# Causal mask of the second score pass: a TensorE mask product or a GpSimd selection on the exponentials

## The chip, the cores and the metric

The kernel runs on one core of one Trainium2 chip. The metric is the device time of one execution in microseconds (us), from launch to the last store. The engines are named as the profile names them: PE is TensorE's matmul, PEld its weight load, DVE is VectorE, ACT is ScalarE, POOL is GpSimd, SP is the DMA queue of SyncE. "L1170" is line 1170 of the kernel before.

## The reference, cut to what matters

The reference is a macaron block on 8 sequences of 512 tokens with 512 features: half a routed feed-forward layer (32 experts, 4 per token), causal attention with 16 heads of 32 features and an ALiBi bias, and half the same feed-forward layer again. The change touches attention alone:

```
x = x + 0.5 * ffn(layernorm(x))
scores = einsum('bqhd,bkhd->bhqk', q, k) * scale + alibi_bias
scores = where(tril(ones(S, S)), scores, -1e9)     # a query sees no later key
p = softmax(scores, axis=-1)
x = x + (p @ v) @ Wout.T + b_out
x = x + 0.5 * ffn(layernorm(x))
```

A "future entry" is a pair of a query and a later key. With 512 tokens cut into tiles of 128, only the diagonal 128x128 square of a key tile's scores holds both kinds; tiles wholly in the future are not computed.

## The kernel before, in words

The program has four stages, one after the other: the routing, the first feed-forward layer, attention (`attend`, L758), the second feed-forward layer. Only `attend` is touched.

**Work units.** `attend` goes through the batches b = 0 to 7 (seven in a hardware loop, the last one written out after it) and in each through four groups g = 0 to 3 of four heads (HG = 4), 32 units in all (u = 4b + g). A unit makes two passes over its scores.

- The first pass (`scores_row`, L1107) computes scores with the queries on the partitions, into `psa`. It is done for the unit after the running one. DVE adds the mask and takes each row's maximum (`maximum`, L1389), PE turns the maxima (`turn_maxima`, L1113), DVE negates them, and two DMAs on ACT's queue (`maxima`, L1278) put them as two more rows into `stq`, so that the second pass subtracts them in the product itself. PE waits for these rows (`s_mr`) at the start of a unit.
- The second pass (`attention`, L1164 to L1187) computes the scores turned, with the keys on the partitions, into `psb`, which has two halves. It runs over the key tiles kt = 0 to 3 and in each over the heads j = 0 to 3, so over n = 4 kt + j = 0 to 15. The tile of kt has the queries from kt * 128 on: 512, 384, 256 and 128 columns. Two products make a tile: the scores (L1168, fp32r, 100 rows), and the mask product (L1170, bf16, 128x128x128: an identity times a matrix with -1e30 at the future entries), which is added to the first 128 columns, the diagonal square. The mask product's semaphore increment (`s_b`) tells ACT, which takes the exponential (`probability`, L1262) of the whole tile into `pt[kt][:, j, :]` and increments `s_e`.
- Between them PE's order is written out by hand: after the scores of n stand, by the tables `A_AT`, `K_AT` and `X_AT`, the next unit's first pass, a quarter of the projection of the keys of the unit after that (`project`, L1080), and in g = 1 the turning of the next batch's rows.

**Two readers of the exponentials.** Both matter here.

- PE's `context(u, g, kt)` (L1128 to L1138) multiplies the values with `pt[kt]` into `psc`, four heads at a time, and increments `s_pv`. It waits until the four exponentials of its key tile are there. It stands in PE's order after the scores of n = 6, 10, 14 for kt = 0, 1, 2 (that is, kt - 1 at j = 2), and after n = 15 for kt = 3.
- POOL's `add_rows(u)` (L994 to L1006) adds `pt[1]`, `pt[2]` and `pt[3]` into `pt[0]`, head by head: four additions of 128x384, four of 128x256, four of 128x128, in that order. The first waits for the context of kt = 0 (`s_pv`), since that reads the old `pt[0]`; each waits for its own exponential. The twelfth releases PE's `sums` (L1140 to L1147, through `s_z`), which adds over the partitions and so gives the softmax's denominators. `sums` of a unit stands in the next unit, behind the first quarter of the projection of the queries (3 matmuls), and for g = 3 behind `values(0)` (12 matmuls). ACT turns the sums into reciprocals (L1269, L1271), DVE multiplies (`normalise`, L1409), and POOL splits the result into a high and a low part (`split_context`, L989 and L991), in the next unit and before that unit's additions.

ACT's exponential n = 0 of a unit waits for the `sums` of the unit before, and the exponentials of kt > 0 for its last addition. After g = 3 POOL has four additions of the bias (L1012), the split, and the stores.

The lines on which it hangs:

```
for kt in range(1, TB):                                        # add_rows, POOL
    for j in range(HG):
        if kt == 1 and j == 0: g.wait_ge(s_pv, u * 4 + 5)
        g.wait_ge(s_e, u * 16 + (kt * HG + j + 2))
        g.tensor_tensor(pt[0][:, j, kt * P:S], ..., pt[kt][:, j, :], ALU.add).then_inc(s_z, 1)
...
pe.wait_ge(s_z, u * 12 + 13)                                   # sums, PE
```

Of the kernel before, what the change touches and what calls it, by code (L numbers as in the profile page):

```python
# [21 lines left out]
P = 128  # L22
ALU = mybir.AluOpType
# [9 lines left out]
B, S, H, HD = 8, 512, 16, 32  # L33
# [724 lines left out]
def attend(nc, tb, d):  # L758
# [5 lines left out]
    NG, HG, TB = H // 4, 4, S // P  # L764
# [11 lines left out]
    DONE_AT = {3: 0, 4: 1, 6: 2, 8: 3}  # L776
    ROW_AT, LOW_AT = {5: 0, 6: 1, 8: 2, 9: 3}, {12: 0, 13: 1, 14: 2, 15: 3}
    RY = TB

    def uses(last):  # L780

# [56 lines left out]
    with ExitStack() as c:  # L838
        sb = lambda n, shape, dt=F32: c.enter_context(nc.sbuf_tensor(f"a_{n}", shape, dt))
        ps = lambda n, shape: c.enter_context(nc.psum_tensor(f"a_{n}", shape, F32))  # L840
        sem = lambda n: c.enter_context(nc.semaphore(f"a_{n}"))
# [2 lines left out]
        wqkv = [sb(f"wqkv_{n}", [P, DC, CQ], F32R) for n in "hl"]  # L844
        wout = [sb(f"wout_{n}", [P, DC, D], F32R) for n in "hl"]
        bqk = sb("bqk", [P, 2 * DC])
        masks, causal = sb("masks", [P, 2, P], BF16), cst[:, C_MQ:C_MK + P].bitcast(BF16)

        stq, stk = sb("stq", [KROWS, 2 * HG, S], F32R), sb("stk", [KROWS, 2 * HG, S], F32R)
# [49 lines left out]
        with nc.Block() as block:  # L899
# [78 lines left out]
            def _(g):  # L978
                def inverse(b, which, mom, rd):
                    g.wait_ge(mom, b + 1)  # L980
                    inverse_deviation(g, s_spare_g, rd, b, st[:, which, :, :], rstd[:, which, :, :])
# [9 lines left out]
                    g.tensor_tensor(ctl[:, g4, :], ct[:, :], cth[:, g4, :].bitcast(F32),  # L991
                                    ALU.subtract).then_inc(s_ch, 1)

                def add_rows(u):  # L994
                    for kt in range(1, TB):
                        for j in range(HG):
                            i = u * 12 + ((kt - 1) * HG + j)
                            if kt == 1 and j == 0:
                                g.wait_ge(s_pv, u * 4 + 5)
                                g.sem_inc(s_spare_g, 1)  # L1000
                            if kt > 1:
                                g.wait_ge(s_z, i - HG + 2)
                                g.sem_inc(s_spare_g, 1)
                            g.wait_ge(s_e, u * 16 + (kt * HG + j + 2))
                            g.tensor_tensor(pt[0][:, j, kt * P:S], pt[0][:, j, kt * P:S], pt[kt][:, j, :],  # L1005
                                            ALU.add).then_inc(s_z, 1)  # L1006
# [19 lines left out]
                def batch(b):  # L1026
                    last = whole(b)
                    for g4 in range(NG):
                        if g4 == 1 and not last:
                            inverse(b + 1, 0, s_mom, s_rd)  # L1030
                        if g4:
                            split_context(b, g4 - 1)
                        add_rows(b * NG + g4)
                    add_bias(b)
                    split_context(b, NG - 1)
                    outputs(b)
# [30 lines left out]
            def _(pe):  # L1067
# [57 lines left out]
                        product(out, [lambda k, x=x: x[:, k, t * P:(t + 1) * P] for x in (cth, ctl)],  # L1125
                                [lambda k, w=w: w[:, k, :] for w in wout], range(DC)).then_inc(s_w, 1)

                def context(u, g, kt):  # L1128

                    pe.wait_ge(s_e, u * 16 + (kt * HG + HG + 1))  # L1130
                    if kt == 0 and not below(u, 2):
                        pe.wait_ge(s_ct, u + 1)
                    for j in range(HG):
                        at = (g * HG + j) * HD
                        mm = pe.matmul(psc[j * HD:(j + 1) * HD, g % 2, kt * P:S], vt[:, kt, at:at + HD],  # L1135
                                       pt[kt][:, j, :], start=(kt == 0), stop=(kt == TB - 1),
                                       skip_group_check=True)
                    mm.then_inc(s_pv, 1)  # L1138
# [10 lines left out]
                def attention(bk, b, g, p_on, a_on, x_on):  # L1149
# [14 lines left out]
                    for kt in range(TB):  # L1164
                        for j in range(HG):
                            n, h = kt * HG + j, (g % 2) * HG + j
                            pe.wait_ge(s_e, u * 16 + n)
                            pe.matmul(psb[:, n % 2, 0:S - kt * P], stk[:, h, kt * P:(kt + 1) * P],  # L1168
                                      stq[:, h, kt * P:S], start=True, stop=False)
                            pe.matmul(psb[:, n % 2, 0:P], masks[:, 0, :], masks[:, 1, :],  # L1170
                                      start=False, stop=True).then_inc(s_b, 1)
                            if a_on and n in A_AT:
                                scores_row(u + 1, (g + 1) % 2, *A_AT[n])
                            if kt and j == 2:
                                context(u, g, kt - 1)
                            if p_on and n in K_AT:
                                k = K_AT[n]
                                if k == 0:
                                    out = take(bk, "k", g)
                                mm = project(out, (g + 2) % NG, 1, (k,))  # L1180
                                if k == DC - 1:
                                    mm.then_inc(s_w, 1)
                            if x_on and n in X_AT:
                                turn_x(bk, b + 1, X_AT[n])
                            if a_on and n == (15 if x_on else 14):
                                turn_maxima(bk, u + 1, g, (g + 1) % 2)
                    context(u, g, TB - 1)  # L1187

                def batch(b):
                    last, bk = whole(b), Bank(b)  # L1190
# [388 lines left out]
```

## Time and profile before

| what | value |
|---|---|
| three timed runs | 2696.55 us median (2694.34 to 2697.74) |
| the profiled execution, its own time | 2696.87 us |
| its span, first to last instruction | 2695.1 us |
| mean granted TensorE clock | 0.966 |
| PE / PEld busy | 2422.7 us (90%) / 1827.9 us (68%) |
| DVE / ACT / POOL busy | 1347.3 us (50%) / 1507.0 us (56%) / 1344.1 us (50%) |
| mask products (L1170) in the trace | 512, mean 238 ns; their weight loads 512, mean 101 ns |
| additions of `add_rows` (L1005) | 384, 266.9 us busy |

The span and the time of the profiled execution lie 1.8 us apart, and that time lies 0.3 us above the median of the timed runs. Busy time is the union of an engine's instructions in an interval; matmuls overlap their neighbours, so the start of one to the start of the next says more of its price than its recorded duration. "Idle before" is the time an engine stood still ahead of an instruction, with the instruction that ended the wait behind the arrow. Where a row of the timeline has "x8" or "x12", that many instructions of one group are merged into it, with the first start and the whole length. The mean granted clock is 1 at 2.4 GHz and 0.5 at 1.2 GHz.

### The profile page before, as it was taken

The numbers are of one execution on the slowest core, as the hardware profiler recorded it, in microseconds if no ns is written. First come the engines' busy times: TensorE is split into PE (matmuls) and PEld (weight loads), VectorE is DVE, ScalarE is ACT, GpSimd is POOL, SyncE is SP. The second block draws the span as 40 slices with busy tenths as digits, with TensorE's granted clock in tenths as the row PEclk, the third lists the DMA queues.
The fourth block names the chain that finished last, engine by engine and source line by source line (L and its number), as shares of the span: only waits on it lengthen the run. The fifth ranks groups of instructions, "written<-read, shape, count | busy, mean of one in ns | idle before, by whom it ended". The sixth has DMA issues, their size and how long they took to land. (4 is left out here: it accounts for less than half of the span.)

```text
span 2695.1 us, 66973 instructions
## 1 busy us (share of the span) xinstructions
PE 2422.7 (90%) x12341; PEld 1827.9 (68%) x12342; DVE 1347.3 (50%) x3658; ACT 1507.0 (56%) x3745; POOL 1344.1 (50%) x1301
## 2 busy tenths in 40 slices
PE   0589999999999759998989989897799999999998
PEld 0268888888888545655656556564588888888886
DVE  8545555555543245455464554642455555555432
ACT  2556666666665425454454544543566666666654
POOL 3146555555555403454444534544356555666554
PEclk9999999999999969999999999996899999999999
DMA  8267877778850132433343333331677777877600
GB/s 296 98 177 176 194 170 171 181 187 186 189 91 0 33 110 64 110 91 94 92 110 97 95 90 108 87 96 39 170 182 178 182 184 168 187 186 183 123 0 1
DMA packets 181221, 348.96 MB, mean 129 GB/s; under 512 B 47143, under 2 KB 98215, under 8 KB 179986
## 3 DMA queue, kind: packets, MB, share of 16 engines
q0 software_dynamic: 76416, 148.62, 26.9%
q1 hardware_dynamic: 93456, 189.91, 24.3%
q10 hardware_dynamic: 11266, 9.61, 1.3%
q14 instruction: 66, 0.54, 0.1%
q8 instruction: 17, 0.28, 0.0%
HBM read 228.24 MB, written 117.96 MB: 128 GB/s over the span
## 5 line engine op out<-in xcount | busy, mean ns | idle before, releaser
L545 PE MATMUL f_psg<-f_wh,f_xh 128*128 x1280 | 535.6, 418 | 5.7 <-DVE f_idle L706 2.8
L545 PE MATMUL f_psg<-f_wh,f_xl 128*128 x1280 | 504.9, 394 | 0.0
L545 PE MATMUL f_psg<-f_wl,f_xh 128*128 x1280 | 502.3, 392 | 0.0
L493 POOL DMA_INDIRECT f_xg<-xn_rows,f_it x320 | 351.4, 1098 | 119.3 <-issue 94.4
L501 POOL DMA_INDIRECT x_rows<-f_ob,f_it x160 | 255.8, 1599 | 298.7 <-ACT f_ob L642 154.0
L501 POOL DMA_INDIRECT out<-f_ob,f_it x160 | 255.6, 1598 | 284.8 <-ACT f_ob L642 129.4
L1389 DVE CUSTOM_DVE_ANT_0 a_psa<-a_psa,cst 128x384 f32<-128x384 f32 (+3 forms) x512 | 249.9, 502 | 246.9 <-PE a_psa L1107 229.3
L1005 POOL TENSOR_TENSOR a_pt<-a_pt 128x256 f32<-128x256 f32 (+2 forms) x384 | 266.9, 733 | 120.3 <-PE a_psc L1135 113.4
L642 ACT ACTIVATE f_ob<-f_pso,f_wcol 128x512 f32<-128x512 f32 x320 | 220.5, 689 | 188.3 <-issue 143.4
L1262 ACT ACTIVATE a_pt<-a_psb 128x256 f32<-128x256 f32 (+3 forms) x512 | 213.3, 437 | 200.9 <-PE a_psb L1170 195.9
L713 DVE TENSOR_TENSOR f_xl<-f_psx,f_xh 128x512 fp32r<-128x512 f32 x320 | 221.3, 692 | 136.9 <-ACT f_xh L623 83.8
L724 DVE TENSOR_TENSOR f_hl<-f_psh,f_hh 128x256 fp32r<-128x256 f32 x320 | 135.9, 425 | 299.3 <-ACT f_hh L649 231.4
L545 PEld LDWEIGHTS f_psg<-f_wh,f_xl 128*128 128x128 f32 x1280 | 241.9, 189 | 57.5
L545 PEld LDWEIGHTS f_psg<-f_wh,f_xh 128*128 128x128 f32 x1280 | 242.4, 189 | 50.0 <-issue 7.9
L545 PEld LDWEIGHTS f_psg<-f_wl,f_xh 128*128 128x128 f32 x1280 | 244.1, 191 | 44.5
L700 DVE TENSOR_TENSOR f_wl<-f_wraw,f_wh 128x768 f32 x256 | 245.4, 960 | 44.6 <-issue 26.7
L559 PE MATMUL f_pso<-f_wh,f_hh 128*128 x640 | 253.2, 396 | 3.0 <-issue 3.0
L559 PE MATMUL f_pso<-f_wl,f_hh 128*128 x640 | 254.8, 398 | 0.0
L559 PE MATMUL f_pso<-f_wh,f_hl 128*128 x640 | 252.8, 395 | 0.0
L610 ACT ACTIVATE f_wh<-f_wraw 128x768 f32 x256 | 215.4, 843 | 57.3 <-DMA f_wraw<-w_in 53.6
L1107 PE MATMUL a_psa<-a_stk,a_stq 98*128 98x384 f32 (+3 forms) x512 | 189.9, 402 | 62.6 <-DVE a_mx L1389 56.0
L630 ACT ACTIVATE f_sg<-f_psg 128x256 f32<-128x256 f32 x320 | 122.9, 384 | 204.8 <-PE f_psg L545 197.1
(193 smaller groups left out, 4357.5 us busy)
## 6 DMA issues: line engine op xcount, KB each, us to landing
f_wraw<-w_in SPq DMA_DIRECT2D x128, 768.0 KB
a_stq<-a_qk SPq DMA_DIRECT2D x128, 144.0 KB
a_stk<-a_qk SPq DMA_DIRECT2D x128, 144.0 KB
r_xt<-x_in SPq DMA_DIRECT2D x8, 1024.0 KB, 14.5
xn_rows<-r_xt SPq DMA_DIRECT2D x8, 1024.0 KB, 4.3
a_xt<-x_rows SPq DMA_DIRECT2D x8, 1024.0 KB, 5.4
a_x<-x_rows SPq DMA_DIRECT2D x8, 1024.0 KB, 5.4
out<-a_x POOLq DMA_DIRECT2D x8, 1024.0 KB, 5.4
```

Of the source, the lines that this page charges most:

```text
L493: g.indirect_dma_start(xg[:, n % XB, :], None, xn_d, bass.IndirectOffsetOnAxis(it[:, n:n + 1], 0), bounds_check=tok_max, oob_is_err=False) ...
L501: g.indirect_dma_start(x_d, bass.IndirectOffsetOnAxis(it[:, n:n + 1], 0), ob[:, n % OB, :], None, bounds_check=tok_max, oob_is_err=False, ...
L545: mm = pe.matmul(psg[:, j, :], x[:, j, k, :], w[:, cols], start=(k == 0 and n == 0), stop=(k == DC - 1 and n == 2))
L559: mm = pe.matmul(pso[:, j, :], h[:, j, k, :], w[:, cols], start=(k == 0 and n == 0), stop=(k == IC - 1 and n == 2))
L610: a.activation(wh[:, ds(at + q * QW, QW)], wraw[r][:, q * QW:(q + 1) * QW], ACT.Copy).then_inc(s_wh[q], 1)
L642: a.activation(ob[:, r, :], pso[:, j, :], ACT.Copy, scale=wcol[:, r:r + 1]).then_inc(s_ob, 1)
L700: ins = v.tensor_tensor(wl[:, cols], wraw[r][:, q * QW:(q + 1) * QW], wh[:, cols].bitcast(F32), ALU.subtract)
L713: v.tensor_tensor(xl[:, j, :, :], psx[:, j, :].rearrange("p (k n) -> p k n", k=DC), xh[:, j, :, :].bitcast(F32), ALU.subtract).then_inc(s_ ...
L1005: g.tensor_tensor(pt[0][:, j, kt * P:S], pt[0][:, j, kt * P:S], pt[kt][:, j, :], ALU.add).then_inc(s_z, 1)
L1107: pe.matmul(psa[:, i % 2, 0:(t + 1) * P], stq[0:3 * HD + 2, h, t * P:(t + 1) * P], stk[0:3 * HD + 2, h, 0:(t + 1) * P], start=True, stop=T ...
L1262: a.activation(pt[kt][:, j, :], psb[:, n % 2, 0:S - kt * P], ACT.Exp).then_inc(s_e, 1)
L1389: v.tensor_tensor_reduce(psa[:, i % 2, 0:(t + 1) * P], psa[:, i % 2, 0:(t + 1) * P], causal[:, S - (t + 1) * P:S], 1.0, 3 * NEG, ALU.add, ...
```

## The change

For most tiles of the second pass the mask product is left out, the score product closes the accumulation and increments `s_b` itself, and the exponentials are taken of unmasked scores in the diagonal square too. A POOL instruction, `affine_select`, then writes zero over the future entries of the first 128 columns of all four heads of one key tile at once (128 partitions x 4 x 128 elements, in place). It waits for the four exponentials of the tile. `context` of such a tile waits for the selection (`s_cut`) in place of the exponentials, and so does the first addition of that key tile on POOL.

`CUT` says which tiles: key tiles 1 and 2 in g = 0, key tiles 0, 1 and 2 in g = 1, 2 and 3; key tile 3 keeps its mask product, and so do key tile 0 of g = 0 and the head j = 0 of every key tile of g = 0. In POOL's order the selection of key tile 0 stands before `split_context`, those of key tiles 1 and 2 right before the four additions of their key tile.

```
+    CUT = ((1, 2), (0, 1, 2), (0, 1, 2), (0, 1, 2))
+    CU = sum(len(kts) for kts in CUT)
+    def cut(b, g, kt):
+        return b * CU + (sum(len(kts) for kts in CUT[:g]) + CUT[g].index(kt) + 1)
...
-                def add_rows(u):
+                def cut_future(b, g4, kt):
+                    g.wait_ge(s_e, (b * NG + g4) * 16 + (kt * HG + HG + 1))
+                    g.sem_inc(s_spare_g, 1)
+                    g.affine_select(pt[kt][:, :, 0:P], pt[kt][:, :, 0:P], [[0, HG], [1, P]], ALU.is_ge, 0.0,
+                                    base=0, channel_multiplier=-1).then_inc(s_cut, 1)
+
+                def add_rows(b, g4):
+                    u = b * NG + g4
                     for kt in range(1, TB):
+                        if kt in CUT[g4]:
+                            cut_future(b, g4, kt)
+                            g.wait_ge(s_cut, cut(b, g4, kt))
+                            g.sem_inc(s_spare_g, 1)
...
+                        if 0 in CUT[g4]:
+                            cut_future(b, g4, 0)
                         if g4:
                             split_context(b, g4 - 1)
-                        add_rows(b * NG + g4)
+                        add_rows(b, g4)
...
-                def context(u, g, kt):
-                    pe.wait_ge(s_e, u * 16 + (kt * HG + HG + 1))
+                def context(b, g, kt):
+                    u = b * NG + g
+                    if kt in CUT[g]:
+                        pe.wait_ge(s_cut, cut(b, g, kt))
+                    else:
+                        pe.wait_ge(s_e, u * 16 + (kt * HG + HG + 1))
...
-                            pe.matmul(psb[:, n % 2, 0:S - kt * P], stk[:, h, kt * P:(kt + 1) * P],
-                                      stq[:, h, kt * P:S], start=True, stop=False)
-                            pe.matmul(psb[:, n % 2, 0:P], masks[:, 0, :], masks[:, 1, :],
-                                      start=False, stop=True).then_inc(s_b, 1)
+                            masked = kt not in CUT[g] or (g == 0 and j == 0)
+                            mm = pe.matmul(psb[:, n % 2, 0:S - kt * P], stk[:, h, kt * P:(kt + 1) * P],
+                                           stq[:, h, kt * P:S], start=True, stop=not masked)
+                            if masked:
+                                mm = pe.matmul(psb[:, n % 2, 0:P], masks[:, 0, :], masks[:, 1, :],
+                                               start=False, stop=True)
+                            mm.then_inc(s_b, 1)
```

## Rows read from the trace of the kernel before

**Rows 1.** The page: busy us (share of the span) xinstructions of each engine.

```profile
PE 2422.7 (90%) x12341; PEld 1827.9 (68%) x12342; DVE 1347.3 (50%) x3658; ACT 1507.0 (56%) x3745; POOL 1344.1 (50%) x1301
```

**Rows 2.** Attention's stretch: length, busy PE, PEld, DVE, ACT, POOL, clock, DMA, GB/s.

```profile
1016.00:1857.00 841.00, 767.19 (x4321) 482.57 (x4319) 435.09 (x1430) 423.43 (x760) 400.73 (x537) 0.96 0.34 93
```

**Rows 3.** PE and PEld's waits in attention: total us, times, longest.

```profile
PE a_psw L1145 <- POOL a_pt L1005: 7.3, 10, 1.5
...
PEld a_psb L1170 <- issue: 50.8, 222, 0.3
```

**Rows 4.** Timeline of PE, group 3, n = 5 (start, length).

```profile
1307.36 0.34 PE L1168 MATMUL a_psb<-a_stq,a_stk 100*128 100x384 f32 x1
1307.54 0.23 PE L1170 MATMUL a_psb<-a_masks 128*128 128x128 bf16 x1
1307.58 0.42 PE L1107 MATMUL a_psa<-a_stk,a_stq 98*128 98x384 f32 x1
1307.84 0.40 PE L1080 MATMUL a_psw<-a_xth,a_wqkv_h 128*128 128x512 f32 x1
```

**Rows 5.** Groups of POOL instructions in attention, shapes apart: busy, mean ns, idle before.

```profile
L1005 POOL TENSOR_TENSOR a_pt<-a_pt 128x384 f32<-128x384 f32 x128 | 125.7, 1013 | 114.1 <-PE a_psc L1135 113.4
L1005 POOL TENSOR_TENSOR a_pt<-a_pt 128x256 f32<-128x256 f32 x128 | 89.1, 729 | 0.0
L1005 POOL TENSOR_TENSOR a_pt<-a_pt 128x128 f32<-128x128 f32 x128 | 54.9, 458 | 6.2 <-ACT a_pt L1262 6.2
```

**Rows 6.** Timeline of POOL, group 2 of the same batch.

```profile
1287.27 0.61 POOL L989 CAST a_cth<-a_ct 128x512 fp32r<-128x512 f32 x1 [10.05 <-DVE a_ct L1409]
1287.96 1.29 POOL L991 TENSOR_TENSOR a_ctl<-a_ct,a_cth 128x512 fp32r<-128x512 f32 x1
1290.58 8.29 POOL L1005 TENSOR_TENSOR a_pt<-a_pt 128x384 f32<-128x384 f32 x12 [1.33 <-PE a_psc L1135]
```

**Rows 7.** Timeline of ACT: exponential n = 7 of groups 0 to 3.

```profile
1245.56 0.93 ACT L1262 ACTIVATE a_pt<-a_psb 128x384 f32<-128x384 f32 x2 [1.06 <-PE a_psb L1170]
...
1268.39 0.93 ACT L1262 ACTIVATE a_pt<-a_psb 128x384 f32<-128x384 f32 x2 [1.11 <-PE a_psb L1170]
...
1290.78 0.94 ACT L1262 ACTIVATE a_pt<-a_psb 128x384 f32<-128x384 f32 x2 [0.86 <-PE a_psb L1170]
...
1310.66 0.94 ACT L1262 ACTIVATE a_pt<-a_psb 128x384 f32<-128x384 f32 x2 [0.61 <-PE a_psb L1170]
```

**Rows 8.** Timeline of PE: `sums` of groups 0 to 3 of that batch.

```profile
1255.45 1.94 PE L1145 MATMUL a_psw<-a_pt,cst 128*32 128x512 f32 x8
...
1279.01 1.06 PE L1145 MATMUL a_psw<-a_pt,cst 128*32 128x512 f32 x8
...
1298.92 1.07 PE L1145 MATMUL a_psw<-a_pt,cst 128*32 128x512 f32 x8 [0.61 <-POOL a_pt L1005]
...
1320.20 1.06 PE L1145 MATMUL a_psw<-a_pt,cst 128*32 128x512 f32 x8
```

**Rows 9.** Timeline of PE: the contexts of key tiles 2 and 3, group 3.

```profile
1315.26 0.64 PE L1135 MATMUL a_psc<-a_pt,a_vt 128*32 128x256 f32 x8
...
1316.86 0.43 PE L1135 MATMUL a_psc<-a_pt,a_vt 128*32 128x128 f32 x8 [0.37 <-ACT a_pt L1262]
```

**Rows 10.** Timeline, group 0 of the batch after: exponential n = 7, `sums`.

```profile
1354.36 0.93 ACT L1262 ACTIVATE a_pt<-a_psb 128x384 f32<-128x384 f32 x2 [1.06 <-PE a_psb L1170]
...
1365.53 1.62 PE L1145 MATMUL a_psw<-a_pt,cst 128*32 128x512 f32 x8
```

**Rows 11.** Timeline, group 1 of the last batch: exponential n = 7, `sums`.

```profile
1809.24 0.81 ACT L1262 ACTIVATE a_pt<-a_psb 128x384 f32<-128x384 f32 x2 [0.98 <-PE a_psb L1170]
...
1817.40 1.94 PE L1145 MATMUL a_psw<-a_pt,cst 128*32 128x512 f32 x8 [1.46 <-POOL a_pt L1005]
```

**Rows 12.** Timeline of PE, group 0: a first-pass product's wait.

```profile
1251.24 0.50 PE L1107 MATMUL a_psa<-a_stk,a_stq 98*128 98x512 f32 x1 [1.66 <-DVE a_mx L1389]
```

**Rows 13.** Busy time, granted clock and DMA of the stretch behind it, as in Rows 2.

```profile
1251.00:1257.00 6.00, 5.27 (x35) 2.20 (x35) 2.22 (x9) 2.02 (x4) 4.57 (x9) 0.76 0.79 185
```

More of the change, by code:

```diff
@@ L846, in attend @@
         bqk = sb("bqk", [P, 2 * DC])
+        s_cut = sem("cut")
         masks, causal = sb("masks", [P, 2, P], BF16), cst[:, C_MQ:C_MK + P].bitcast(BF16)
@@ L1174, in attention @@
                             if kt and j == 2:
-                                context(u, g, kt - 1)
+                                context(b, g, kt - 1)
                             if p_on and n in K_AT:
@@ L1186, in attention @@
                                 turn_maxima(bk, u + 1, g, (g + 1) % 2)
-                    context(u, g, TB - 1)
+                    context(b, g, TB - 1)
                 def batch(b):
```

## The prediction

> **What bounds the kernel now.** I read the page first: PE is busy nine tenths of the span, POOL half [rows 1]. The change lies in attention alone, so the busy times of that stretch come next: of 841 us PE works 767 and POOL 401 [rows 2]. By these shares PE is the bound, and POOL has room for more. But shares don't tell who waits for whom. The waits show PE standing for POOL's additions ahead of `sums` (10 times in the records, up to 1.5 us) [rows 3]. The timeline says where: in group 2 the twelve additions run 8.29 us from 1290.58, to 1298.87 [rows 6], and `sums` starts at 1298.92, after 0.61 us of idle [rows 8]. So group 2 is set by POOL's chain already. In the other groups `sums` comes later than that chain for reasons of PE's order (12 matmuls of `values` behind group 3, the turned rows and DVE's statistics in groups 0 and 1). PE is in order: whatever delays `sums` or a context delays all behind it.
>
> **The gain: mask products.** Per batch 42 of 64 go (6 in group 0, 12 in each other), so 336 in all; 176 stay. Their price is read from starts [rows 4]. The 384-column scores take 0.18 us to the next start (1307.36 to 1307.54), the mask 0.04, and the 384-column product behind it 0.26, that is 0.08 more than the scores, because its weights were not there yet. So a mask costs 0.12 us. The bounds are 0.04 (its own step) and 0.23 (its recorded length). If all were on PE's path: 336 * 0.12 = 40 us. The trace shows PEld idle ahead of the mask's load ("issue", 50.8 us in 222 places) [rows 3]. The Trainium skill's page "TensorE: Matmul & The Clock Gate" (Part 2, "What happens when you issue a matmul") says that the engine pulls weight loads ahead of running matmuls; by that rule a mask would cost its 0.04 alone, and all of them 13 us. The trace doesn't bear it out for these loads, so I keep 0.12.
>
> Of a unit, 8 masks stand before the end of exponential n = 7 (in group 0 only the three of n = 5 to 7 go). The saving of n = 3 is lost in a wait for DVE's maximum, so 7 * 0.12 = 0.84; besides, the increment comes from the scores themselves, some 0.08 earlier. So exponential 7 ends s = 0.9 us earlier in groups 1 to 3, and 3 * 0.12 + 0.08 = 0.45 in group 0. With a mask's bounds s lies between 0.3 and 1.7.
>
> **The price: 88 selections** (11 a batch) of 128x512 elements. The trace has none. The nearest rows from both sides are POOL's cast of 128x512, one input, 0.61 us, and its subtraction of 128x512, two inputs, 1.29 [rows 6]. A selection reads one input but must compute an index and compare for each element; I take the middle, D = 0.95. The total, 88 * 0.95 = 84 us, would fit into POOL's idle time. It is the place that counts:
>
> - Key tile 0's selection (groups 1 to 3) has from the fourth exponential to the context of key tile 0 some 2.7 us; hidden up to there. It delays `split_context` by 0.1 us or nothing.
> - Key tile 1's waits for exponential 7, and the additions behind it. Until now they started at the end of context 0: 1290.58, before exponential 7 had ended (1290.78 + 0.49 = 1291.27 [rows 7], two merged into the row).
> - Key tile 2's stands behind key tile 1's four additions. Its share of the 8.29 us is 1013 / (1013 + 729 + 458) of it = 3.82 [rows 5]. PE's context 2 waits for it.
>
> So POOL's new chain from the end of exponential 7 (E7) is: 0.08 to notice, D, 0.08 to the additions (the gap from cast to subtraction [rows 6]), 3.82, D, 0.08, 4.47, and 0.05 to `sums`: 8.6 + 2D = 10.5 us. Against the old `sums` [rows 7, 8]:
>
> - Group 2: 1291.27 - 0.9 + 10.5 = 1300.87, was 1298.92: +1.95.
> - Group 3: 1311.15 - 0.9 + 10.5 = 1320.75, was 1320.20: +0.55. But context 2 may start only at E7 + 0.16 + 3.82 + 2D + 0.08 = E7 + 5.96 = 1316.2, was 1315.26 [rows 9]: +0.95. From there to context 3 it was 1.6, now 1.35 (one mask less, and DVE's maxima are no longer awaited). That moves context 3, and `sums` with it, by +0.7.
> - Group 1: 1268.88 - 0.9 + 10.5 = 1278.48, was 1279.01: -0.5 (PE alone, with its context 2 moved, would give -0.7).
> - Group 0: 1246.05 - 0.45 + 10.5 = 1256.1, was 1255.45: +0.65. Every other batch the old `sums` is later: exponential 7 at 1354.36 + 0.49, `sums` at 1365.53 [rows 10]. There it gives 1364.9: -0.6. On average 0.
>
> A full batch: 1.95 + 0.7 - 0.5 + 0 = +2.15, seven of them +15 us. The last batch lacks the next one's projections and turned rows, and all its groups hang on POOL. Its group 1: exponential 7 ends at 1809.24 + 0.49 = 1809.73, so 1809.73 - 0.9 + 10.5 = 1819.3, was 1817.40 [rows 11]: +1.9; four such, +7.6. Together +22.7.
>
> **Other edits.** Late next: the turned maxima stand behind context 2, up to 1 us later, while the next unit starts behind a `sums` that is later still; nothing. SP's stacks wait for score products two units ahead: nothing; if that cover went, the same lateness of about 1 us a unit would show. After group 3 POOL's bias and split end 1.8 us later, PE has three tiles of `values` (36 matmuls) in between: nothing. The added semaphore steps are in the 0.08.
>
> **The clock.** In group 0 PE waits 1.66 us for DVE [rows 12], and the stretch behind it has a granted clock of 0.76 [rows 13], so part of it is at 1.2 GHz. Group 2 will have two waits of about 2 us each (context 2, `sums`). What a longer slow stretch costs is seen in group 0: from E7 to `sums` 10.68 us with the longer, 9.40 with the shorter, so 1.3 more [rows 7, 8, 10]. If each group 2 got one: 8 * 1.3 = 10; partly hidden behind POOL. I take 4.
>
> **Sum.** 22.7 + 4 = 27 on the profiled execution's 2696.87, which is 0.3 above the median: 2724 us.
>
> **Rivals.** What a measurement can tell here is about 0.2%, 5.4 us.
>
> - *The selection is as fast as a cast* (D = 0.61). Chain 9.8: group 2 +1.27, group 3 about 0, group 1 -0.9 (then PE's own order holds), group 0 -0.35; times seven 0, last batch 4 * 1.2 = 5, half of the clock 2: 2702 to 2704, at the edge of no change. For it: one input. Against: the comparison. The Trainium skill's page "GPSIMD Engine Reference" (7, "Performance pitfalls for Q7 kernels") gives compare-and-select bodies 1.03 cycles an element when unrolled, 2.03 when not; my estimate from that is 0.44 or 0.87 us for 512 elements at its 1.2 GHz, without start-up. The first would lead to this rival's time.
> - *Faster: POOL's chain gets shorter by more than the selections lengthen it.* The mechanism is E7: at a mask's recorded 0.23 us s = 1.7, with D = 0.61 the chain gives group 2 1291.27 - 1.7 + 9.8 = 1299.4 (+0.5), group 1 -2, group 0 -0.4, group 3 -0.9; -2.8 a batch, last batch +2: -18, 2679 us. It decides where 2D - s falls below about 0.3 (it is 1.0 in my sum, and each 1.0 is worth some 32 units, 32 us). For it: PE is the busiest engine. Against: the starts say 0.12.
> - *The selection is slower than a subtraction*: D = 2 adds 2 * 1.05 in each of 32 units, 67 us: 2791. The rows can't exclude it, since no such instruction is among them. At D = 1.29: 2724 + 0.34 * 2 * 32 = 2746.
>
> That the masks aren't dropped is excluded by the code.
>
> **Chances.** My forecast and its surroundings (D 0.75 to 1.3) 0.52; a cast's pace 0.2, half of it within 0.2%; dearer masks 0.16, of which 0.03 end within 0.2%; a slower selection 0.12. So faster 0.13, same 0.13, slower 0.74. The range goes from 2690 (towards a cast's pace and dearer masks) to 2758 (D = 1.29 with all of the clock's 10 us and some more), and leaves out about 0.2.
>
> **What would show it.** Right: 176 mask products; group 2's first addition about 0.8 us later than before, measured from the unit's start, and `sums` 2 us later; a new wait of PE for `pt` ahead of the context of key tile 2, about 2 us in groups 2 and 3; a selection of 0.8 to 1.1 us; the feed-forward stages unchanged. Wrong: if the idle time ahead of context 2 is nil, or exponential 7 comes over 1.5 us earlier, or a selection takes as long as a cast or over 1.3 us.

## The result and the profile after

The changed kernel takes 2755.88 us (median of 4 runs, 2751.51 to 2758.79), the kernel before on the same chip 2697.14; the ratio is 1.0201 with a 95% interval of [1.0185, 1.0218]. It is slower by 58.7 us, inside the range forecast (2690 to 2758), but more than twice the 27 us of the forecast itself. The span of the profiled execution grew by the same, 2753.8 - 2695.1 = 58.7 us.

The page of the changed kernel, its engines, and the stretch of attention (columns as in [rows 2]):

```profile
PE 2428.9 (88%) x12005; PEld 1836.2 (67%) x12006; DVE 1339.3 (49%) x3658; ACT 1503.7 (55%) x3745; POOL 1397.6 (51%) x1389
```

```profile
1016.00:1916.00 900.00, 774.07 (x3989) 490.79 (x3988) 427.28 (x1430) 420.33 (x760) 453.64 (x624) 0.90 0.32 87
```

The feed-forward stages kept their length; attention took all of it. PE lost its 336 instructions (12341 to 12005) and is yet busy longer, since its mean clock in attention fell from 0.96 [rows 2] to 0.90. POOL worked 53 us more in attention and is still half idle. PE's waits there, in the same columns as [rows 3]:

```profile
PE a_psa L1128 <- DVE a_mx L1417: 43.3, 75, 2.1
PE a_psc L1160 <- POOL a_pt L1005: 32.2, 25, 1.8
PE a_psw L1170 <- POOL a_pt L1024: 18.9, 16, 3.0
```

The wait for DVE is the old one (40.2 us in the kernel before). New is the context's wait for the selection (L1005 now), 32.2 us, and the wait of `sums` for the additions (L1024) went from 7.3 [rows 3] to 18.9. These 44 us are only a part; a unit shows the rest. POOL in group 2 of the third batch, the counterpart of [rows 6] (the unit starts at 1298.28; start, length, [idle before]):

```profile
1302.27 0.63 POOL L1005 TENSOR_SCALAR_AFFINE_SELECT a_pt<-a_pt 128x512 f32<-128x512 f32 x1 [8.29 <-ACT a_pt L1290]
1302.97 0.61 POOL L996 CAST a_cth<-a_ct 128x512 fp32r<-128x512 f32 x1
1303.67 1.29 POOL L998 TENSOR_TENSOR a_ctl<-a_ct,a_cth 128x512 fp32r<-128x512 f32 x1
1306.72 0.64 POOL L1005 TENSOR_SCALAR_AFFINE_SELECT a_pt<-a_pt 128x512 f32<-128x512 f32 x1 [1.76 <-ACT a_pt L1290]
1307.76 3.88 POOL L1024 TENSOR_TENSOR a_pt<-a_pt 128x384 f32<-128x384 f32 x4 [0.41 <-POOL a_pt L1005]
1311.59 0.64 POOL L1005 TENSOR_SCALAR_AFFINE_SELECT a_pt<-a_pt 128x512 f32<-128x512 f32 x1
1312.63 4.43 POOL L1024 TENSOR_TENSOR a_pt<-a_pt 128x256 f32<-128x256 f32 x8 [0.41 <-POOL a_pt L1005]
```

A selection takes 0.64 us, as long as the cast, but 0.41 us of idleness follow each that has additions behind it. The first addition starts at 1307.76, 9.48 us into the unit; it was 8.39, and 0.8 more was forecast. And PE in the same unit, from the last scores but one on:

```profile
1310.45 0.23 PE L1197 MATMUL a_psb<-a_masks 128*128 128x128 bf16 x1
1312.28 0.64 PE L1160 MATMUL a_psc<-a_pt,a_vt 128*32 128x256 f32 x8 [1.60 <-POOL a_pt L1005]
1312.85 0.28 PE L1134 MATMUL a_psw<-cst,a_mx 128*16 128x128 f32 x1
...
1313.63 0.66 PE L1160 MATMUL a_psc<-a_pt,a_vt 128*32 128x128 f32 x8 [0.37 <-ACT a_pt L1290]
1314.21 0.80 PE L1101 MATMUL a_psw<-a_xth,a_wqkv_h 128*128 128x512 f32 x1
1314.81 0.63 PE L1101 MATMUL a_psw<-a_xtl,a_wqkv_h 128*128 128x512 f32 x1
1315.23 0.63 PE L1101 MATMUL a_psw<-a_xth,a_wqkv_l 128*128 128x512 f32 x1
1317.12 1.93 PE L1170 MATMUL a_psw<-a_pt,cst 128*32 128x512 f32 x8 [1.25 <-POOL a_pt L1024]
1318.98 0.80 PE L1101 MATMUL a_psw<-a_xth,a_wqkv_h 128*128 128x512 f32 x1
1319.58 0.62 PE L1101 MATMUL a_psw<-a_xtl,a_wqkv_h 128*128 128x512 f32 x1
```

Two things are to be seen. Context 2 stands 1.60 us for the selection of key tile 2, and `sums` 1.25 us for the twelfth addition. And what PE does between and behind them is slow: projection products of 512 columns follow each other in 0.42 us, not 0.23, and `sums` takes 1.93 us, where it took 1.07 [rows 8]. The granted clock is at its lower level (1.2 GHz) for more than half of both stretches: its mean is 0.73 from 1310 to 1317 us and 0.69 from 1317 to 1322 (columns as in [rows 2]):

```profile
1310.00:1317.00 7.00, 3.90 (x27) 1.90 (x27) 1.83 (x7) 2.02 (x4) 6.59 (x11) 0.73 0.74 173
1317.00:1322.00 5.00, 4.88 (x20) 2.68 (x20) 0.00 (x0) 2.51 (x3) 0.06 (x1) 0.69 0.28 69
```

In group 3 the twelve products of `values` meet the same, so `sums` comes 4.9 us after context 3, not 3.3.

The unit lengths below are means of seven batches, from the starts of the scores n = 0 in each trace; the last column gives, for each group, the us of such a unit during which the granted clock was at 1.2 GHz ("slow clock" from here on).

| kernel | group 0 | group 1 | group 2 | group 3 | slow clock in groups 0, 1, 2, 3 |
|---|---|---|---|---|---|
| before | 24.8 | 22.8 | 19.9 | 41.5 | 5.4, 0.5, 0, 0 |
| after | 25.6 | 23.2 | 23.5 | 43.5 | 7.8, 2.0, 6.8, 3.4 |

Group 2 lost 3.6 us, group 3 2.0, the others 0.8 and 0.4: 6.8 a batch, 48 us in seven; the last batch lost 10 more, and the start of the first unit came 1.0 later.

### The profile page after: what moved, and what is told of

It is laid out like the page before. It is cut to its first block and busy times, and to the rows that moved or that the text cites. A ratio compares the mean times of both kernels' runs of the same rounds, so it can differ in the third digit from the quotient of the medians.

```text
span 2753.8 us, 66682 instructions
## 1 busy us (share of the span) xinstructions
PE 2428.9 (88%) x12005; PEld 1836.2 (67%) x12006; DVE 1339.3 (49%) x3658; ACT 1503.7 (55%) x3745; POOL 1397.6 (51%) x1389
## 3 DMA queue, kind: packets, MB, share of 16 engines
q1 hardware_dynamic: 93456, 189.91, 23.6%
## 5 line engine op out<-in xcount | busy, mean ns | idle before, releaser
L1024 POOL TENSOR_TENSOR a_pt<-a_pt 128x256 f32<-128x256 f32 (+2 forms) x384 | 265.9, 728 | 25.2 <-POOL a_pt L1005 21.8
L700 DVE TENSOR_TENSOR f_wl<-f_wraw,f_wh 128x768 f32 x256 | 245.3, 959 | 43.5 <-issue 26.7
L1128 PE MATMUL a_psa<-a_stk,a_stq 98*128 98x384 f32 (+3 forms) x512 | 170.7, 367 | 66.4 <-DVE a_mx L1417 58.9
```

Of the source, the lines that this page charges most:

```text
L700: ins = v.tensor_tensor(wl[:, cols], wraw[r][:, q * QW:(q + 1) * QW], wh[:, cols].bitcast(F32), ALU.subtract)
L1128: pe.matmul(psa[:, i % 2, 0:(t + 1) * P], stq[0:3 * HD + 2, h, t * P:(t + 1) * P], stk[0:3 * HD + 2, h, 0:(t + 1) * P], start=True, stop=T ...
```

## The experiments

Each ratio is to runs of the kernel before made beside the experiment; their medians lie between 2698.2 and 2700.7 us. Where two changed kernels are compared, the difference of their medians and that of their ratios can lie some ten microseconds apart, so a gain of ten is uncertain by as much. Unit lengths and slow clock come from the one execution that was traced.

**A selection that is off the path.** The first question is which selections cost. Only key tile 0 is selected:

```
-    CUT = ((1, 2), (0, 1, 2), (0, 1, 2), (0, 1, 2))
+    CUT = ((), (0,), (0,), (0,))
```

> Edit: CUT = ((), (0,), (0,), (0,)); only key tile 0 of groups 1 to 3 is selected, 96 mask products go, 24 selections come. Theory (the loss comes from the selections of key tiles 1 and 2, which stand in POOL's chain to the sums, and from the clock that falls in PE's waits for it): the selection of key tile 0 is hidden, in the changed kernel it ends at 4.63 us of the unit and context 0 starts at 6.3. Four masks less move context 0 and the first addition by 0.4 us in 24 units: 10 us less than the kernel before, 2687, clock as before (0.96 in attention). Rival (any selection on POOL costs, by delaying the split of the context or by disturbing DVE): no gain or a loss against the kernel before, 2697 or more.

Measured: 2702.4 us, ratio 1.0010 [0.9995, 1.0024] to the kernel before. The total fits the rival, the units don't: groups 2 and 3 are 0.4 us shorter, as the theory has it, but group 1 has 23.6 us (22.8 before) and group 0 25.5. There more time lies at 1.2 GHz (2.9 us, 0.5 before, in group 1). An example is group 0 of the fourth batch, 29.5 us long. PE there, behind the wait for DVE at the batch's start that the kernel before has too:

```profile
1346.76 0.79 PE L1128 MATMUL a_psa<-a_stk,a_stq 98*128 98x128 f32 x2 [1.75 <-DVE a_mx L1417]
1347.35 0.73 PE L1101 MATMUL a_psw<-a_xth,a_wqkv_h 128*128 128x512 f32 x1
1347.88 0.63 PE L1101 MATMUL a_psw<-a_xtl,a_wqkv_h 128*128 128x512 f32 x1
1348.31 0.63 PE L1101 MATMUL a_psw<-a_xth,a_wqkv_l 128*128 128x512 f32 x1
```

In the traces the clock stays up behind this wait in every batch of the kernel before, and here in every batch but the fourth. So a second theory was needed beside POOL's chain: PE's waits let the clock fall, in some executions of the same wait and not in others, and that costs more than the wait.

**The masks alone.** No selection; 336 mask products left out, the future entries of those tiles not zeroed, and the exponentials of a quarter of the scores:

```
-                            cut_future(b, g4, kt)                     # and cut_future(b, g4, 0)
-                            g.wait_ge(s_cut, cut(b, g4, kt))
-                            g.sem_inc(s_spare_g, 1)
...
-                    if kt in CUT[g]:
-                        pe.wait_ge(s_cut, cut(b, g, kt))
+                    pe.wait_ge(s_e, u * 16 + (kt * HG + HG + 1))
...
-                                 ACT.Exp).then_inc(s_e, 1)
+                                 ACT.Exp, scale=0.25).then_inc(s_e, 1)
```

> Edit: the 336 mask products are left out as in the changed kernel, but no selection is made and contexts and additions wait for the exponentials as before; the future entries of these tiles are not zeroed, and the exponentials are taken of a quarter of the scores, so that the sums stay in range. It prices the masks alone. Theory (a mask costs about 0.12 us of PE's order, part of it lost in waits for DVE): exponential 7 ends 0.8 us earlier, units shorter by 0.7 to 1.2 us: 2697 - 32 * 0.8 = 2671, down to 2665. Rival 1 (a mask costs its recorded 0.23 us): 2697 - 50 to 70 = 2640. Rival 2 (fewer columns on PE let the granted clock fall by themselves): slower than 2690, with a clock in attention below 0.94.

Measured: 2691.1 us, ratio 0.9968 [0.9953, 0.9984]. A miss of 20 us for the theory. The first rival is out. The second isn't: it named a time over 2690 us and a clock in attention under 0.94, and the trace has 0.94 (0.96 before), so this run stands at both of its bounds. Exponential 7 of group 2 ends 0.80 us earlier than before, as the theory has it, but of the gain little is left: units of groups 2 and 3 are 0.7 and 0.9 us shorter, those of groups 0 and 1 1.0 and 0.1 longer, with 8.8 and 2.0 us of slow clock (5.4 and 0.5 before). There is no selection here to wait for. PE's waits for DVE in attention are longer, in the same columns as [rows 3]; they were 40.2 us in 71 places:

```profile
PE a_psa L1124 <- DVE a_mx L1410: 48.4, 82, 2.1
```

Against the changed kernel it says that the selections, their waits and the clock behind them cost 65 us in all.

**Masks and selections both.**

```
-                            masked = kt not in CUT[g] or (g == 0 and j == 0)
+                            masked = True
```

> Edit: the changed kernel with all 512 mask products kept (masked = True); the selections and their waits stay. Theory: exponential 7 ends 0.8 us later again, POOL's chain starts from it, so each unit is 0.8 us longer than in the changed kernel: 2756 + 26 = 2782. Rival (the clock falls because PE has less work without the masks, and not because it waits): the clock of attention comes back towards 0.96 and the time falls below 2750.

Measured: 2788.5 us (2778.4 to 2798.2), ratio 1.0340 [1.0302, 1.0377], in the direction of the chain theory (2782). The trace is of the fastest of these executions, 2778.4 us. Group 2 still has 8.2 us of slow clock, more than the changed kernel's 6.8. So in group 2 it isn't the lesser work without masks that lets the clock fall. For groups 0 and 1 this run doesn't decide: their slow clock is 9.2 and 0.6 us (7.8 and 2.0 in the changed kernel).

**Useless work in the waits.** The clock can be told from the waits by giving PE something to do in them that no result uses:

```
+                def fill(n):
+                    for _ in range(n):
+                        pe.matmul(psb[:, 1, :], wqkv[0][:, 0, 0:P], wout[0][:, 0, :], start=True, stop=True)
...
+                    if kt == 2 and g >= 1:                            # in context
+                        pe.wait_ge(s_e, (b * NG + g) * 16 + 15)
+                        fill(5)
...
+                    fill((0, 5, 8, 0)[g])                             # in sums
                     pe.wait_ge(s_z, u * 12 + 13)
```

> Edit: the changed kernel with useless products in PE's waits for POOL: 5 of 128x128x512 ahead of the context of key tile 2 in groups 1 to 3 (after a wait for exponential n = 13), 5 ahead of the sums that stand in group 2 of the order and 8 ahead of those called for group 2, into the idle half of psb. No result changes. Theory (part of the loss, about half, is the granted clock at 1.2 GHz behind the waits: 1.4 us behind the sums in group 2, 1.5 in the values of group 3, 0.5 in groups 0 and 1 each per batch): the clock of attention rises from 0.90 to 0.96 and the time falls by 20 to 30 us, to 2726 to 2736, though PE has more to do. Rival (the loss is waiting alone, the clock only falls in waits and costs nothing): 2756 or some us more.

Measured: 2753.3 us, ratio 1.0194 [1.0168, 1.0221]: by its total the rival's. But groups 2 and 3 are 22.1 and 42.2 us, 1.5 and 1.3 shorter than in the changed kernel, without any slow clock, and all of that was lost again: in group 1 (24.6; its wait is short, and the products themselves moved context 2 by 1.35 us), in group 0 (26.8, with 10.7 us of slow clock) and in the last batch (5.3 us longer). So they were put only where the wait is:

```
-                    if kt == 2 and g >= 1:
+                    if kt == 2 and g >= 2:
...
-                    fill((0, 5, 8, 0)[g])
+                    if g == 2:
+                        fill(8)
```

> Edit: as e5_fill, with the useless products only where it helped there: 5 ahead of the context of key tile 2 in groups 2 and 3, 8 ahead of group 2's sums. In e5_fill group 2 and 3 became 1.33 us shorter each and groups 1 and 0 longer (context 2 of group 1 1.35 us later by the products themselves). Theory (behind those waits the clock at 1.2 GHz costs 1.3 us a time in groups 2 and 3): groups 2 and 3 as in e5_fill, groups 0 and 1 as in the changed kernel: 2756 - 7 * 2.7 = 2737. Rival (the clock falls somewhere else instead, in groups 0 and 1): under 8 us gained, 2748 or more.

Measured: 2733.0 us, ratio 1.0149 [1.0111, 1.0188], against the changed kernel's 2755.9: 23 us less for more work on PE. Three of the four executions took 2730.4 to 2734.0 us, the fourth 2747.9, so by the ratios the gain is 14 us; by the unit lengths of the trace (groups 2 and 3 are 1.5 and 1.3 us shorter, groups 0 and 1 as in the changed kernel) it is 20 in seven batches. The same stretch of group 2 as above (the unit starts 4.85 us earlier):

```profile
1306.02 1.43 PE L1151 MATMUL a_psb<-a_wout_h,a_wqkv_h 128*128 128x512 f32 x5 [0.18 <-ACT a_pt L1299]
1307.47 0.64 PE L1167 MATMUL a_psc<-a_pt,a_vt 128*32 128x256 f32 x8
1308.82 0.43 PE L1167 MATMUL a_psc<-a_pt,a_vt 128*32 128x128 f32 x8 [0.37 <-ACT a_pt L1299]
...
1312.34 1.07 PE L1179 MATMUL a_psw<-a_pt,cst 128*32 128x512 f32 x8 [0.30 <-POOL a_pt L1024]
1313.34 0.50 PE L1101 MATMUL a_psw<-a_xth,a_wqkv_h 128*128 128x512 f32 x1
1313.67 0.39 PE L1101 MATMUL a_psw<-a_xtl,a_wqkv_h 128*128 128x512 f32 x1
1313.90 0.40 PE L1101 MATMUL a_psw<-a_xth,a_wqkv_l 128*128 128x512 f32 x1
```

`sums` starts at the same point of the unit, 18.91 us in (18.84 in the changed kernel), since POOL sets it; it takes 1.07 us again, and the projection behind it goes at 0.23 us a product. That is the clock's share in groups 2 and 3, shown by itself.

**Key tile 0 once more**, from the other side: masks for it in all groups, key tiles 1 and 2 selected.

```
+    CUT = ((1, 2), (1, 2), (1, 2), (1, 2))
```

> Edit: CUT = ((1, 2), (1, 2), (1, 2), (1, 2)): key tile 0 keeps its mask products everywhere, key tiles 1 and 2 are selected, so 96 masks more than in the changed kernel and 24 selections less. Theory: exponential 7, from which the chain starts, comes 0.4 us later in 24 units, 2756 + 10 = 2766, so key tile 0's selection is no part of the loss. Rival (it is a part of it): 2750 or less.

Measured: 2766.7 us, ratio 1.0261 [1.0238, 1.0284], 10.8 more than the changed kernel. Key tile 0's selection, with the masks that it saves, is a gain; the loss is with key tiles 1 and 2.

**The hand-over behind a selection.**

```
+                            if kt == 1:
+                                g.wait_ge(s_pv, u * 4 + 5)
+                            else:
+                                g.wait_ge(s_z, u * 12 + ((kt - 1) * HG - HG + 2))
+                            g.sem_inc(s_spare_g, 1)
                             cut_future(b, g4, kt)
-                            g.wait_ge(s_cut, cut(b, g4, kt))
-                            g.sem_inc(s_spare_g, 1)
...
+                            if j == 0 and kt in CUT[g4]:
+                                g.wait_ge(s_cut, cut(b, g4, kt))      # the addition itself waits
```

> Edit: in add_rows of the changed kernel the wait for the context (key tile 1) or for the earlier addition (key tile 2) stands ahead of the selection, and the first addition behind a selection waits for s_cut itself, without the semaphore instructions that stood between the two. Same work, same order. In the changed kernel 0.41 us lie between the end of a selection and the first addition, where cast and subtraction have 0.08. Theory (the gap is the hand-over through semaphore instructions, and POOL's chain from exponential 7 to the sums is what counts): gaps of about 0.1, sums 0.6 us earlier in each of 32 units: 2756 - 20 = 2736. Rival (POOL needs 0.4 us to change from this instruction to another): no change, 2756.

Measured: 2744.9 us (2736.8 to 2747.4), ratio 1.0182 [1.0160, 1.0205]. POOL in group 2 (the unit starts at 1289.48):

```profile
1297.92 0.63 POOL L1005 TENSOR_SCALAR_AFFINE_SELECT a_pt<-a_pt 128x512 f32<-128x512 f32 x1 [1.76 <-ACT a_pt L1298]
1298.64 1.00 POOL L1022 TENSOR_TENSOR a_pt<-a_pt 128x384 f32<-128x384 f32 x1
```

The gap is 0.09 us instead of 0.41, so it was the semaphore instructions between; `sums` comes 0.64 us earlier in the unit (18.20 us in). The medians lie 11 us apart, not 20, and the interval overlaps the changed kernel's. The traced execution is the fastest of the four, 2736.8 us, what was expected; in it groups 1 to 3 are 0.5 to 0.6 us shorter each, and group 0 is 0.2 longer, with more slow clock (8.8 us, 7.8 in the changed kernel). The other three took 2743.0 to 2747.4, and what they lost isn't shown.

**Context 2 earlier.**

```
                         if kt in CUT[g4]:
-                            cut_future(b, g4, kt)
+                            if kt == 1:
+                                cut_future(b, g4, kt)
                             g.wait_ge(s_cut, cut(b, g4, kt))
...
+                            if kt == 1 and j == 1:
+                                cut_future(b, g4, 2)
```

> Edit: in the changed kernel the selection of key tile 2 moves ahead, between the second and the third addition of key tile 1. Same work. It tells the wait ahead of context 2 from the wait ahead of the sums. Theory: context 2 of groups 2 and 3 starts 1.8 us earlier (12.2 us of the unit, not 14.0), its wait of 1.6 us goes; the sums gain 0.3 by the hidden hand-over in every unit, and those of group 3, behind PE's values, about 1.7; with one wait of two gone less time at 1.2 GHz behind it. Per batch 0.3 + 0.3 + 1 + 1.7 = 3.3: 2756 - 26 = 2730. Rival (the sums are the only place that counts): 32 * 0.3 = 10 us, 2746.

Measured: 2773.1 us, ratio 1.0285 [1.0263, 1.0307]: 17 us slower than the changed kernel, and expected by neither theory. Group 3 did as expected (41.8 us, 43.5 before the edit; context 2 at 12.3 us of the unit): with its wait ahead of context 2 gone, its 3.4 us of slow clock are gone too. But POOL is in order, and in group 1, where PE has the turned rows between, exponential 11 comes late; POOL in that group:

```profile
1289.07 1.97 POOL L1025 TENSOR_TENSOR a_pt<-a_pt 128x384 f32<-128x384 f32 x2 [0.41 <-POOL a_pt L1005]
1292.33 0.63 POOL L1005 TENSOR_SCALAR_AFFINE_SELECT a_pt<-a_pt 128x512 f32<-128x512 f32 x1 [1.29 <-ACT a_pt L1293]
1292.93 6.34 POOL L1025 TENSOR_TENSOR a_pt<-a_pt 128x384 f32<-128x384 f32 x10
```

The selection stands 1.29 us, with two additions behind it that had their data. `sums` comes 0.9 us later, at the end of one longer wait of PE (context 3 starts at 16.1 us of the unit, `sums` at 20.3). Group 1 is 25.5 us long with 5.4 at 1.2 GHz, group 0 27.5 with 12.6.

**Chain and clock together.** The two edits that helped, the hand-over's diff above and in it:

```
+                    if kt == 2 and g >= 2:                            # in context
+                        pe.wait_ge(s_e, (b * NG + g) * 16 + 15)
+                        fill(5)
...
+                    if g == 2:                                        # in sums
+                        fill(6)
```

> Edit: e4_handover and the useless products of e8_fill_g23 together (5 ahead of context 2 in groups 2 and 3, 6 ahead of group 2's sums). Theory (chain and clock are separate terms and add up): 2745 - 22 = 2723; what is left over the kernel before, 25 us, is POOL's chain through two selections, about what I had forecast. Rival (they are one term): 2733, as e8_fill_g23.

Measured: 2723.7 us, ratio 1.0076 [1.0055, 1.0097]. Against the hand-over alone the products gain 21 us (29 by the ratios), so the two terms add up, as the theory has it; groups 2 and 3 have no slow clock here either.

**The clock in the kernel before.** PE has two waits for DVE in its group 0, of about 1.7 us each, at n = 1 (from the third batch on) and at n = 12 [rows 12]. In the trace its 5.4 us of slow clock there lie behind the second [rows 13]. Useless products in both, in no other place, and all masks as they were:

```
+                            if g == 0 and n == 1:
+                                pe.wait_ge(s_ct, u + 1)
+                                fill(psc[:, 0, :], 8)
+                            if g == 0 and n == 12:
+                                pe.wait_ge(s_e, u * 16 + 13)
+                                fill(psb[:, 1, :], 6)
```

> Edit: the kernel before (all masks, no selection) with useless products in PE's two waits for DVE in group 0: 8 of 128x128x512 ahead of the first-pass product at n = 1, into the idle half of psc, and 6 at n = 12, into the idle half of psb. No result changes. In the kernel before 5.4 us of each group 0 lie at 1.2 GHz, behind these waits. Theory (the clock that falls in these waits costs about 1 us a batch, more when it falls at the start of the batch): clock of attention near 1, 2697 - 7 to 12 = 2688. Rival (the clock falls elsewhere in its place, or the products delay PE): 2697 or more.

Measured: 2689.8 us, ratio 0.9960 [0.9943, 0.9978]. Group 0 is 23.3 us, with no slow clock; the other groups as before. The same lines then went into the kernel with key tile 0's selections alone:

```
+    CUT = ((), (0,), (0,), (0,))
...
+                                fill(psc[:, 0, :], 8)
...
+                                fill(psb[:, 1, :], 6)
```

> Edit: e1_kt0_only (selections of key tile 0 in groups 1 to 3 alone) with the useless products of e9_before_fill0. In e1_kt0_only groups 2 and 3 became 0.39 us shorter each, as expected, but group 1 got 2.9 us at 1.2 GHz where the kernel before has 0.5, and became 1.1 us longer in five of seven batches. Theory (that was the clock, not the selection): with the clock held in group 0, groups 1 to 3 are each 0.4 us shorter than in the kernel before, 8 us less than e9_before_fill0: 2680. Rival (key tile 0's selection costs group 1 something): equal to e9_before_fill0 or slower.

Measured: 2680.2 us (2679.6 to 2680.6), ratio 0.9919 [0.9900, 0.9939] to the kernel before: the fastest of the kernels that compute the reference. Groups 1, 2 and 3 are 0.6, 0.4 and 0.4 us shorter than in the kernel with the products alone. Here the selection that the change brings does gain: 9.6 us for 24 of them and the 96 masks that they save.

And into the kernel without selections and without 336 masks:

```
-                            cut_future(b, g4, kt)
...
+                                 ACT.Exp, scale=0.25).then_inc(s_e, 1)
...
+                                fill(psc[:, 0, :], 8)
...
+                                fill(psb[:, 1, :], 6)
```

> Edit: e2_no_select (no selections, 336 masks left out, exponentials of a quarter of the scores) with the useless products of e9_before_fill0. In e2_no_select groups 2 and 3 were 0.7 and 0.85 us shorter, groups 0 and 1 not. Theory (there too the masks' time was saved, but the clock took it back): against e9_before_fill0 each batch is 0.7 + 0.85 + 0.5 + 0.4 = 2.5 us shorter, 20 us: 2668. Rival (in groups 0 and 1 the masks cost nothing, since PE waits for DVE there): 2688 - 12 = 2676 or more.

Measured: 2671.3 us, ratio 0.9886 [0.9867, 0.9906]; as in the other kernel without selections, future entries are not zeroed. Against 2689.8 the 336 masks are worth 18.5 us, 0.055 each. Groups 1 to 3 are 1.0, 0.5 and 0.7 us shorter than with the products alone, group 0 is not (23.4). So the theory (2668) holds for groups 1 to 3 and the rival for group 0. It also answers the clock rival of the kernel without selections: with the waits of group 0 filled, groups 1 to 3 have the lesser work without masks and at most 0.5 us of slow clock each.

## Why the prediction was wrong

**The place was right.** The changed kernel has 176 mask products, the wait ahead of context 2 in groups 2 and 3 is there (1.60 us in the rows above), group 2's `sums` starts 18.84 us into its unit, where 18.68 was forecast, against 16.73 before. POOL's chain from exponential 7 through two selections to the additions sets it: 10.56 us, forecast 10.5. Keeping masks, dropping key tile 0's selection and shortening the hand-over moved the time in the direction that this chain says: +33, +11 and -11 us, where +26, +10 and -20 were expected from it.

**Two of its terms were mis-sized and cancelled.** The selection has 0.64 us, not 0.95, so my bound by the subtraction was far off and the one by the cast right. The Trainium skill's page "GPSIMD Engine Reference" (7, "Performance pitfalls for Q7 kernels") had led me to estimates of 0.44 us without start-up by its unrolled figure and 0.87 by the other; the measured 0.64 lies under the second, so it fits only the unrolled one. But the hand-over from selection to addition has 0.41, where I took cast to subtraction (0.08) for its like. That row had one wait on the subtraction itself; here separate semaphore instructions stood between, and the experiment that removed them got 0.09. Two selections at 0.31 less and two gaps at 0.33 more leave the chain as it was; that the chain came out at 10.56 us is luck. By a rule that I had written myself, a selection as fast as a cast, I would have expected no change.

**The masks.** The price of 0.12 us each nearly held in PE's order in groups 2 and 3: exponential 7 of group 2 ends 8.28 us into the unit, 0.80 earlier (0.9 forecast), which by the same sum is 0.10 a mask. The Trainium skill's page "TensorE: Matmul & The Clock Gate" (Part 2, "What happens when you issue a matmul") has weight loads pulled ahead of running matmuls, and the 0.04 us a mask by that rule would give 7 * 0.04 + 0.08 = 0.36 us, too little for this 0.80. Over the whole kernel a mask is worth 0.055 us, since a part goes into waits (those for DVE grew from 40.2 to 48.4 us when the masks alone were left out); the "40 us if all were on PE's path" were not there to be had.

**The step that failed is the clock.** I wrote: "If each group 2 got one: 8 * 1.3 = 10; partly hidden behind POOL. I take 4." Those 4 us are the term that was mis-sized: in groups 2 and 3 alone the clock was worth 20 us by the unit lengths and 23 by the medians. For group 2 by itself the 10 us of that line were right; the discount to 4 was wrong, and the other groups had no term. The slow clock grew from 5.9 to 20.0 us a batch, and in every group:

- In group 2 the projection behind `sums` isn't hidden behind anything: its unit took 3.6 us more, forecast 1.95, and useless products in its two waits gave 1.5 back.
- Group 3 I didn't have at all. Its `sums` stands behind 12 products of `values`, right after context 2's wait; I counted them at full speed and got +0.7. It became +2.0, and the products in the waits gave 1.3 back.
- In groups 0 and 1 the forecast was 0 and -0.5, measured +0.8 and +0.4. A part isn't the clock: exponential 7 ends 0.2 and 0.55 us earlier there, not 0.45 and 0.9, so `sums` stands 0.5 us later in group 0 and only 0.1 earlier in group 1. The time at 1.2 GHz rose by 2.4 and 1.5 us. The waits for POOL aren't needed for this rise: without any selection the kernel with its masks left out has 8.8 and 2.0 us of slow clock, the changed kernel 7.8 and 2.0. So it comes with the masks that are left out; the longer waits for DVE are a likely path, and it isn't shown that they are the one.

Filled waits in groups 2 and 3 took off these 23 us by an edit that leaves masks, selections and additions as they are. With it 2733 remain, against a forecast of 2724 with 4 us of clock in it. Of the 9 to 13 us between, the last batch accounts for 2 (10 lost, 7.6 forecast), and the rest lies in groups 0 and 1, whose units are 1.6 us a batch longer than forecast. How much of that is the clock no experiment isolated in the changed kernel.

That 2755.9 lies inside the range is luck too: the upper end stood for a selection of 1.29 us with 10 us of clock, and neither was so.

The rivals: the faster one is out by the masks' price. The "slower than a subtraction" one (2746 to 2791) had about the right sum for a wrong reason.

## What to carry to other kernels

An engine half idle over the whole kernel is no room for work that enters a chain between two waits of the bound engine. Walk that chain from the last event that it starts from to the one that it releases, and count the semaphore instructions in it.

When an edit gives the tensor engine new waits, price work behind them at half the clock, not only the waits: here one long wait of 1.6 us a unit (group 3) had 3.4 us of slow clock behind it, and two waits (group 2) had 6.8. And when an edit's unit-by-unit gains don't show in the total, look at the time at the lower clock in the units that were not edited: the kernel with key tile 0 alone measured 2702, and 2680 once two old waits were filled (of which the filling alone gives 7 to 11).

## What was not expected of the hardware

- Useless products in PE's waits made five kernels faster: 2755.9 to 2733.0, 2744.9 to 2723.7, 2697.1 (2700.7 beside it) to 2689.8, 2702.4 to 2680.2 and 2691.1 to 2671.3 us. PE did more work in less time, with fewer microseconds at 1.2 GHz behind the waits. In one more kernel, where they also stood ahead of a short wait, they gained nothing (2753.3).
- The same wait, 1.7 to 1.9 us at n = 1 of group 0, was followed by the lower clock in one batch of the kernel with key tile 0 alone and not in its other four: from the third batch on its group 0 took between 24.9 and 29.5 us with identical instructions. Filled, it took 23.4 to 23.6. In the kernel with products in groups 1 to 3 (2753.3 us) the clock fell behind this wait in all five.
- A GpSimd selection over 128x512 numbers takes 0.64 us, as its one-input cast (0.61); the semaphore instructions between it and its reader cost half as much again (0.41 us against 0.09).
